# One core: skip term summed by TensorE, products read from PSUM, 7 of 32 weighings on GpSimd, direct SiLU and GELU in the end groups

## Chip, core and metric

The kernel runs on one core of a Trainium2 chip. The metric is the device time of one execution in microseconds (us), the median of repeated runs. TensorE (PE) multiplies matrices into PSUM, VectorE (DVE), ScalarE (ACT) and GpSimd (POOL) do elementwise work, SyncE (SP) issues the DMAs.

## The reference

x is 32 sequences of 128 tokens by 128 features, all float32. One layer of it:

```python
x = x + attn(rotate(x))            # rotate: pairs of rows turned by an angle per sequence
x = x + ffn(lora(x))
# attn: layernorm, then _mamba forward and on the reversed sequence, then
xc = conv4(xi) + conv_b;  u = silu(xc);  dbc = u @ x_proj.T
delta = softplus(dt @ dt_proj.T + b)           # B, C: 16 states each
h = exp(delta * A) * h + (delta * u) * B       # a scan over the tokens
y = sum_n(h * C) + u * D                       # u * D is the skip term
y = y * silu(z) @ out_proj.T
y = gelu([y_fwd, y_rev] @ reduce.T + b);  g = y @ glu.T + glu_b
attn = g[:128] * sigmoid(g[128:]) + rotate(x)
# lora: relu(x @ Wi[expert]) @ Wo[expert]
# ffn:  h = silu(x @ w1 * s1) * (x @ w2 * s2); h = gelu(h @ h1 * s); h = gelu(h @ h2 * s); h @ w3 * s
```

The inner width of the scan is 256 (two halves of 128 partitions), there are 16 states and two directions.

## The kernel before, in words

The 32 sequences are worked in nine groups: the first and the last hold two sequences (256 tokens wide), the seven between hold four (512 wide). In a group a "unit" is one state of one direction, so a group has 32 units: 16 forward (d=0), 16 reversed (d=1). A unit is a pipeline over the engines:

- GpSimd `drive`: state = du * B, L471. 128x1024 elements in a full group (two halves of 512).
- ScalarE `decays`: exp(delta * A) into one of two PSUM tiles (`bank_d`), two instructions of L614. It waits until the unit two before is done with the tile.
- VectorE `scan`: h = decay * h + state. Its result goes back into PSUM (L797) where VectorE multiplies by C next, or into SBUF (L795) where GpSimd does.
- `weigh`: times C, on VectorE from PSUM (L802) or on GpSimd (L476). The table `POOL_UNITS` names the units of a group that GpSimd weighs: 9 of 32.
- TensorE `sum_states`: eight 128x128 transposes (four in a narrow group) that add the product into `bank_y`, turned, L1076.

After 16 units a direction is finished: ScalarE copies `bank_y` to `ysum` (`copy_y`, L620), TensorE turns it back into `bank_y` (`turn_y`, L1084), VectorE adds u * D (`take_y`, two instructions, L810) into `ysum`, and then multiplies by silu(z) (`gate_y`, L819). `bank_y` is free for the other direction when `take_y` is done, and eight state buffers (`RING`) go round, so `drive` waits for the sums.

Beside the units run the "fills": matmuls of the other stages into two PSUM tiles `bank_m`, each followed by a "take" on ScalarE or VectorE that reads it. For a group: norm, uf0 uf1 ur0 ur1 (projection and convolution in one, L921), z0 z1, dbc0 dbc1, dt.., out, glu0 glu1, res, hid0-3, wo, gate0-3, up0-3, h1_0-3 (L991), h2_0-3 (L997), w3 (L1003), tok. SiLU and GELU run over whole tiles after plain takes (L570 on u, L575 on the gate, L665 on the two hidden layers), in one instruction each, to change ScalarE's table seldom: exponentials need another table than SiLU or GELU, and each change is a table load (L502).

The order of each engine's queue is fixed by tables of numbers. A time axis counts units; `FILL`, `TAKE_LAG`, `ACT_AT`, `VEC`, `GPS`, `TURN` and `LOADS` say at which unit of its group, relative to the group's first unit, each step stands. A back end of group g (FILL 37.5 to 74) runs beside the units of group g+1. Every engine walks the same axis and issues what stands there, so a shifted number moves an instruction to another place in a queue; semaphores keep the order right. SP issues the loads of B and C rows, of the weights chosen by expert (`load_selected`) and the stores in the same way.

## Time and profile before

| | us |
|---|---|
| median of 3 runs | 1112.93 (1109.14 to 1113.81) |
| the profiled execution | 1111.34 |
| its span, first to last instruction | 1109.5 |
| TensorE busy | 932.5 |
| VectorE busy | 927.7 |
| GpSimd busy | 883.1 |
| ScalarE busy | 809.0 |
| mean granted TensorE clock | 0.937 of full speed |

Busy is the time in which an instruction of the engine ran. A float32 matmul shows as two records, and so "x8" of such a line is four matmuls; a transpose is one record. Neighbouring instructions overlap by some 0.08 us, so a row's mean is that much more than what the next one waits for.

### The profile page before, as it was taken

The page shows a single profiled execution, that of the slowest core. Times are in us where ns is not written, and L with a number is a line of the kernel's source. Part 1 is how long each engine was busy: PE and PEld are TensorE (multiplying, and loading weights), DVE is VectorE, ACT ScalarE, POOL GpSimd, SP SyncE. Part 2 cuts the span into 40 slices and gives each one's busy share as a digit, 9 for nine tenths or more (in the row PEclk, how much of TensorE's full clock was granted, in tenths as well). Part 3 has the DMA queues.
Part 4 walks back from the last instruction along what each step waited for, and adds up shares of the span by engine and source line. Part 5 has one row for each costly group of instructions (what it writes and reads, how often), then busy time and mean ns, then how long its engine had stood idle before and what let it go on. Part 6 is the DMA issues. An engine that isn't in the chain of part 4 may idle for free.

```text
span 1109.5 us, 13685 instructions
## 1 busy us (share of the span) xinstructions
PE 932.5 (84%) x4240; PEld 591.1 (53%) x4240; DVE 927.7 (84%) x734; ACT 809.0 (73%) x1265; POOL 883.1 (80%) x448
## 2 busy tenths in 40 slices
PE   3498568876989989998999899998999779978876
PEld 2255345654655547545755465555655565546445
DVE  1577899999998999989998999899999999778410
ACT  3845675879688877878687968887788758676552
POOL 0675999999989898989988998899899988666200
PEclk9598679888999999999999999999999989989999
DMA  5446855465536555474536653755447453445100
GB/s 184 127 149 163 251 175 172 118 231 168 149 103 230 165 159 154 126 232 133 170 114 208 177 167 90 243 163 163 139 143 237 141 169 97 144 107 113 50 10 5
DMA packets 100840, 167.45 MB, mean 151 GB/s; under 512 B 12320, under 2 KB 36320, under 8 KB 100512
## 3 DMA queue, kind: packets, MB, share of 16 engines
q1 hardware_dynamic: 100768, 166.58, 49.5%
q8 instruction: 34, 0.56, 0.2%
...
## 4 chain that ended last, share of the span: by engine, by line
PE 36%; DVE 25%; ACT 16%; issue 16%; POOL 4%; SPq 2%; DMA 1%; DVEq 0%; ACTq 0%; POOLq 0%
DVE bank_d L797 15%; PE bank_y L1076 8%; PE bank_m L997 8%; PE bank_m L991 6%; ACT bank_d L614 5%; PE bank_m L921 4%; DVE state L795 4%; ACT L502 2%; POOL state L471 2%; PE bank_m L1003 2%; PE bank_m L933 2%; PE bank_m L939 2%; ACT hidA L665 1%; PE bank_m L953 1%; ACT hidB L665 1%
## 5 line engine op out<-in xcount | busy, mean ns | idle before, releaser
L471 POOL TENSOR_TENSOR state<-du,b_rows 128x1024 f32<-128x1024 f32 (+1 forms) x288 | 618.3, 2167 | 77.4 <-PE bank_y L1076 64.0
L797 DVE TENSOR_TENSOR_SCAN bank_d<-bank_d,state 128x1024 f32<-128x1024 f32 (+1 forms) x207 | 424.2, 2049 | 49.2 <-ACT bank_d L614 48.7
L614 ACT ACTIVATE bank_d<-delta,a_neg 128x512 f32<-128x512 f32 (+1 forms) x576 | 343.6, 633 | 82.8 <-DVE state L802 68.7
L1076 PEld LDWEIGHTS bank_y<-ident,state 128*128 128x128 f32 x2048 | 244.4, 147 | 129.6 <-issue 88.3
L1076 PE MATMUL bank_y<-ident,state 128*128 128x128 f32 x2048 | 275.1, 283 | 33.0 <-POOL state L476 16.9
L802 DVE TENSOR_TENSOR state<-bank_d,c_rows 128x1024 f32<-128x1024 f32 (+1 forms) x207 | 228.8, 1105 | 10.7 <-DMA c_rows<-bc_store 3.7
L476 POOL TENSOR_TENSOR state<-state,c_rows 128x1024 f32<-128x1024 f32 (+1 forms) x81 | 175.3, 2164 | 19.4 <-DVE state L795 18.0
L795 DVE TENSOR_TENSOR_SCAN state<-bank_d,state 128x1024 f32<-128x1024 f32 (+1 forms) x81 | 165.4, 2042 | 3.6 <-ACT bank_d L614 3.5
L997 PE MATMUL bank_m<-hidA,h_s 128*128 128x512 f32 (+1 forms) x288 | 126.1, 586 | 23.2 <-ACT hidA L665 23.2
L991 PE MATMUL bank_m<-hidB,h_s 128*128 128x512 f32 (+1 forms) x288 | 117.7, 554 | 16.2 <-DVE hidB L839 15.9
L921 PE MATMUL bank_m<-xnT,w_conv 128*128 128x508 f32 (+7 forms) x288 | 119.0, 559 | 2.0 <-ACT xnT L548 1.8
L502 ACT ACT_TABLE_LOAD x84 | 107.8, 1283 | 2.3 <-PE bank_m L953 0.8
L997 PEld LDWEIGHTS bank_m<-hidA,h_s 128*128 128x128 f32 x288 | 56.8, 207 | 72.1 <-issue 70.1
L991 PEld LDWEIGHTS bank_m<-hidB,h_s 128*128 128x128 f32 x288 | 53.2, 194 | 64.8 <-issue 40.2
L921 PEld LDWEIGHTS bank_m<-xnT,w_conv 128*128 128x128 f32 x288 | 54.5, 197 | 49.4 <-issue 43.4
L451 POOL TENSOR_TENSOR delta<-relu_dt,log_dt 128x1024 f32<-128x1024 f32 (+1 forms) x18 | 38.2, 2121 | 29.3 <-ACT log_dt L605 29.3
L659 ACT ACTIVATE hidB<-bank_m,col 128x512 f32<-128x512 f32 (+1 forms) x36 | 22.9, 635 | 43.7 <-PE bank_m L997 43.5
L953 PE MATMUL bank_m<-gy,w_glu_s 128*128 128x512 f32 (+1 forms) x36 | 23.3, 736 | 36.9 <-ACT gy L624 36.1
L939 PE MATMUL bank_m<-dbc,w_dt_s 64*128 64x512 f32 (+1 forms) x72 | 38.7, 626 | 11.6 <-ACT dbc L589 8.0
L655 ACT ACTIVATE hidA<-bank_m,col 128x512 f32<-128x512 f32 (+1 forms) x36 | 22.8, 632 | 31.6 <-PE bank_m L991 31.6
L982 PE MATMUL bank_m<-glu_a,w_s 128*128 128x512 f32 (+1 forms) x72 | 36.3, 621 | 9.1 <-ACT glu_a L649 8.2
L558 ACT ACTIVATE u_r<-bank_m,col 128x512 f32<-128x512 f32 (+1 forms) x18 | 11.5, 639 | 41.0 <-PE bank_m L921 41.0
(112 smaller groups left out, 989.9 us busy)
## 6 DMA issues: line engine op xcount, KB each, us to landing
b_rows<-bc_store SPq DMA_DIRECT2D x224, 256.0 KB, 4.7
c_rows<-bc_store SPq DMA_DIRECT2D x224, 256.0 KB, 4.7
...
```

What stands on the lines that cost most here:

```text
L471: nc.gpsimd.tensor_tensor(split(unit_state(u)), du[:, d, :, :width(g)], per_half(b_rows, u), ALU.mult).then_inc(S.bx_ready, 1)
L476: nc.gpsimd.tensor_tensor(split(unit_state(u)), split(unit_state(u)), per_half(c_rows, u), ALU.mult).then_inc(S.weighed, 1)
L502: act.preload_act_table_set(name)
L614: ins = act.activation(split(unit_decay(u))[:, h], delta[:, d, h, :width(g)], ACT.Exp, scale=a_neg[:, h, n:n + 1])
L795: dve.tensor_tensor_scan(drive, decay, drive, 0.0, ALU.mult, ALU.add).then_inc(S.unit_done, 1)
L797: dve.tensor_tensor_scan(decay, decay, drive, 0.0, ALU.mult, ALU.add).then_inc(S.scanned, 1)
L802: dve.tensor_tensor(split(unit_state(u)), split(unit_decay(u)), per_half(c_rows, u), ALU.mult).then_inc(S.unit_done, 1)
L921: ins = pe.matmul(dst, w, src, start=(m == 0), stop=(m == TAPS - 1))
L939: return pe.matmul(bank(g, f"dt{d}{h}"), w_dt_s[:, h * P:(h + 1) * P], dbc[0:DTR, :width(g)], start=True, stop=True)
L991: ins = pe.matmul(bank(g, f"h1_{f}"), h1_s[:, q, f * P:(f + 1) * P], hidB[:, q, :width(g)], start=(q == 0), stop=(q == FC - 1))
L997: ins = pe.matmul(bank(g, f"h2_{f}"), h2_s[:, q, f * P:(f + 1) * P], hidA[:, q, :width(g)], start=(q == 0), stop=(q == FC - 1))
L1076: ins = pe.matmul(bank_y[:, h, s * P:(s + 1) * P], split(unit_state(u))[:, h, s * LEN:(s + 1) * LEN], ident[:, :], start=(n == 0 and s == ...
```

## The change

1. The skip term. `take_y` goes. `skip` is a new constant of two 128x128 matrices diag(D), made on VectorE at the start (`skip_weights`). `turn_y` first multiplies it with u into `bank_y` (one matmul per half), then adds the turned sums to it. `gate_y` reads `bank_y` from PSUM and multiplies by silu(z) at once, for d=1 with both patterns reversed; `bank_y` is free when it is done.
2. The gated linear unit: `glu0` is no longer copied by ScalarE (L631); VectorE's `add_skip` reads it from PSUM and adds its bias while it multiplies.
3. `POOL_UNITS` has 7 units in place of 9: two weighings per group go from GpSimd to VectorE.
4. In group 0 the takes of u apply SiLU themselves, and in group 8 the takes of gate, h1 and h2 apply SiLU and GELU themselves; their whole-tile instructions are gone there.
5. The selected weights are loaded one sequence at a time at four places of the axis. `tok` and `cT` share a buffer.
6. All tables of the axis have other numbers, and `slot` adds offsets of its own for group 0 (`FIRST_GROUP`) and group 8 (`LAST_GROUP`).

```diff
-POOL_UNITS = (1, 4, 8, 11, 14, 18, 22, 25, 29)
+POOL_UNITS = (3, 8, 12, 17, 21, 26, 30)
...
-TURN = (19.0, 34.0)
+TURN = (19.0, 36.0)
...
-LOADS = {"x": -37.5, "bc_store": (-8.5, 0.0), "selected": 29.5, "store": 77.0}
+LOADS = {"x": -38.5, "bc_store": (-7.5, 0.0), "selected": (24.0, 26.0, 28.0, 30.0), "store": 78.0}
...
+def slot(table, g, name, k=None):
+
+    at = table[name] if k is None else table[name][k]
+    if g == 0:
+        return at + FIRST_GROUP.get(name, 0.0)
+    return at + LAST_GROUP.get(name, 0.0) if g == NG - 1 else at
...
+        def wait_u(eng, g, d):
+            if g == 0:
+                wait_taken(eng, g, *(("uf0", "uf1"), ("ur0", "ur1"))[d])
+            else:
+                eng.wait_ge(S.u_ready, 2 * (g - 1) + d + 1)
+
+        def wait_hidden(eng, g, name):
+
+            if g == NG - 1:
+                wait_taken(eng, g, *all_of(name))
+            else:
+                eng.wait_ge({"gate": S.gate_ready, "h1_": S.h1_ready, "h2_": S.h2_ready}[name], g + 1)
...
-                return act.activation(dst if d == 0 else dst[:, ::-1], bank(g, name), ACT.Identity, bias=c("conv_b", h))
+                if g == 0:
+                    use_table(SILU)
+                return act.activation(dst if d == 0 else dst[:, ::-1], bank(g, name), ACT.Silu if g == 0 else ACT.Identity, bias=c("conv_b", h))
...
             def take_wo(g):
+
+                wait(act, S.stored, 16 * g)
                 return act.activation(cT[:, :width(g)], bank(g, "wo"), ACT.Copy)
...
-                return act.activation(hidA[:, f, :width(g)], bank(g, f"h1_{f}"), ACT.Copy, scale=c("h1_s", f))
+                if g == NG - 1:
+                    use_table(GELU)
+                return act.activation(hidA[:, f, :width(g)], bank(g, f"h1_{f}"), ACT.Gelu if g == NG - 1 else ACT.Copy, scale=c("h1_s", f))
...
+            def skip_weights():
+                dve.wait_ge(S.ident_ready, 1)
+                for h in range(HALVES):
+                    ins = dve.tensor_scalar(skip[:, h], ident[:, :], c("skip_d", h), None, ALU.mult)
+                ins.then_inc(S.skip_ready, 1)
...
-            def take_y(g, d):
+            def gate_y(g, d):
                 dve.wait_ge(S.y_turned, 2 * g + d + 1)
-                wait(dve, S.gated_ready, 2 * g + d)
-                w = width(g)
-                for h in range(HALVES):
-                    dst = ysum[:, h, :w] if d == 0 else ysum[:, h, :w][:, ::-1]
-                    ins = dve.scalar_tensor_tensor(dst, (u_f, u_r)[d][:, g % 2, h, :w], c("skip_d", h), bank_y[:, h, :w], ALU.mult, ALU.add)
-                ins.then_inc(S.y_taken, 1)
...
-                dve.tensor_tensor(gated[:, d, :, :w], ysum[:, :, :w], z[:, g % 2, :, :w], ALU.mult).then_inc(S.gated_ready, 1)
+                dst, gate_z = gated[:, d, :, :w], z[:, g % 2, :, :w]
+                if d == 1:
+                    dst, gate_z = dst[:, :, ::-1], gate_z[:, :, ::-1]
+                dve.tensor_tensor(dst, bank_y[:, :, :w], gate_z, ALU.mult).then_inc(S.gated_ready, 1)
...
-                dve.tensor_tensor(x1T[:, :w], glu_a[:, :w], glu_t[:, :w], ALU.mult).then_inc(S.x1_ready, 1)
+                dve.scalar_tensor_tensor(x1T[:, :w], bank(g, "glu0"), c("glu_b", 0), glu_t[:, :w],
+                                         ALU.add, ALU.mult).then_inc(taken_of(g, "glu0"), 1)
...
-                    wait(pe, S.y_taken, 2 * g + d)
+                    wait(pe, S.gated_ready, 2 * g + d)
...
+                wait(pe, S.skip_ready, 1)
+                w = width(g)
                 for h in range(HALVES):
+                    pe.matmul(bank_y[:, h, :w], skip[:, h], (u_f, u_r)[d][:, g % 2, h, :w], start=True, stop=False, skip_group_check=True)
                     for s in range(sequences(g)):
-                        ins = pe.transpose(bank_y[:, h, s * LEN:(s + 1) * LEN], y_rows[:, h, s * P:(s + 1) * P], ident[:, :])
+                        ins = pe.matmul(bank_y[:, h, s * LEN:(s + 1) * LEN], y_rows[:, h, s * P:(s + 1) * P], ident[:, :],
+                                        start=False, stop=True, is_transpose=True, skip_group_check=True)
```

The other take functions of the last group change as `take_h1` does. What the new numbers do to the queues is shown at three places. The first is TensorE where the units of group 4 begin and the back end of group 3 is in its second hidden layer (L991 h1, L997 h2, L1076 sums, L1084 the turning, L946 out). Before:

```order
L991 MATMUL bank_m<-hidB,h_s 128x512 x4
L1076 MATMUL bank_y<-ident,state 128x128 x24
L997 MATMUL bank_m<-hidA,h_s 128x512 x4
L1076 MATMUL bank_y<-ident,state 128x128 x8
L997 MATMUL bank_m<-hidA,h_s 128x512 x4
L933 MATMUL bank_m<-u_r,w_x_s 96x512 x2
L1076 MATMUL bank_y<-ident,state 128x128 x8
L939 MATMUL bank_m<-dbc,w_dt_s 128x512
L1076 MATMUL bank_y<-ident,state 128x128 x8
L997 MATMUL bank_m<-hidA,h_s 128x512 x4
L939 MATMUL bank_m<-dbc,w_dt_s 128x512
L1084 MATMUL bank_y<-ident,ysum 128x128 x8
```

The same place in the changed kernel (L1029 h1, L1114 sums, L1035 h2, L1123 and L1125 the new turning, L984 out):

```order
L1029 MATMUL bank_m<-hidB,h_s 128x512 x12
L1114 MATMUL bank_y<-ident,state 128x128 x32
L971 MATMUL bank_m<-u_r,w_x_s 96x512 x2
L1114 MATMUL bank_y<-ident,state 128x128 x8
L1035 MATMUL bank_m<-hidA,h_s 128x512 x4
L977 MATMUL bank_m<-dbc,w_dt_s 128x512
L1114 MATMUL bank_y<-ident,state 128x128 x16
L977 MATMUL bank_m<-dbc,w_dt_s 128x512
L1035 MATMUL bank_m<-hidA,h_s 128x512 x8
L1123 MATMUL bank_y<-u_r,skip 128x512
L1125 MATMUL bank_y<-ident,ysum 128x128 x4
L1123 MATMUL bank_y<-u_r,skip 128x512
```

Between the last h1 fill and the first h2 fill there stood 24 transposes; now 40 and the two dbc matmuls stand there. The turning has two matmuls more and comes after three h2 fills, as before.

The second is ScalarE a little later, from the last take of h2 on (L659 take of h2, L665 GELU, L537 and L541 the layernorm of the group after next, L624 `gy`, the GELU of out, L614 decays). Before:

```order
L659 ACTIVATE hidB<-bank_m,col 128x512
L614 ACTIVATE bank_d<-delta,a_neg 128x512 x2
L502 ACT_TABLE_LOAD
L665 ACTIVATE hidB<-hidB 128x2048
L537 ACTIVATE shift<-neg_mean,rstd 128x1 x4
L541 ACTIVATE scaled<-xc,shift,rstd 128x128 x4
L502 ACT_TABLE_LOAD
L614 ACTIVATE bank_d<-delta,a_neg 128x512 x4
L502 ACT_TABLE_LOAD
L624 ACTIVATE gy<-bank_m,col 128x512
L502 ACT_TABLE_LOAD
L614 ACTIVATE bank_d<-delta,a_neg 128x512 x2
```

The changed kernel (L570 and L574 layernorm, L698 take of h2, L650 decays, L704 GELU, L660 `gy`):

```order
L570 ACTIVATE shift<-neg_mean,rstd 128x1 x4
L574 ACTIVATE scaled<-xc,shift,rstd 128x128 x4
L698 ACTIVATE hidB<-bank_m,col 128x512
L650 ACTIVATE bank_d<-delta,a_neg 128x512 x4
L535 ACT_TABLE_LOAD
L704 ACTIVATE hidB<-hidB 128x2048
L660 ACTIVATE gy<-bank_m,col 128x512
L535 ACT_TABLE_LOAD
L650 ACTIVATE bank_d<-delta,a_neg 128x512 x2
```

The layernorm stands ahead of the take, and `gy` directly behind the GELU of h2, so that one pair of table loads is gone.

The third is ScalarE at the end of the program, the back end of group 8 (L655 and L659 takes of h1 and h2, L575 SiLU of the gate, L652 take of the gate). Before:

```order
L649 ACTIVATE glu_a<-bank_m 128x256
L652 ACTIVATE hidA<-bank_m,col 128x256 x4
L502 ACT_TABLE_LOAD
L575 ACTIVATE hidA<-hidA 128x4x256
L655 ACTIVATE hidA<-bank_m,col 128x256 x4
L502 ACT_TABLE_LOAD
L665 ACTIVATE hidA<-hidA 128x4x256
L659 ACTIVATE hidB<-bank_m,col 128x256 x4
L665 ACTIVATE hidB<-hidB 128x4x256
```

The changed kernel:

```order
L682 ACTIVATE cT<-bank_m 128x256
L535 ACT_TABLE_LOAD
L687 ACTIVATE hidA<-bank_m,col 128x256 x4
L535 ACT_TABLE_LOAD
L692 ACTIVATE hidA<-bank_m,col 128x256 x4
L698 ACTIVATE hidB<-bank_m,col 128x256 x4
```

Each table load stands ahead of the four takes, and three whole-tile instructions are gone.

## Rows read from the trace of the kernel before

**Rows 1.** The page: busy us of each engine, and the chain by engine.

```profile
PE 932.5 (84%) x4240; PEld 591.1 (53%) x4240; DVE 927.7 (84%) x734; ACT 809.0 (73%) x1265; POOL 883.1 (80%) x448
...
PE 36%; DVE 25%; ACT 16%; issue 16%; POOL 4%; SPq 2%; DMA 1%; DVEq 0%; ACTq 0%; POOLq 0%
```

**Rows 2.** Stretches: length, busy of PE, PEld, DVE, ACT, POOL, clock, DMA.

```profile
43.20:119.00 75.80, 62.82 (x259) 40.10 (x258) 60.99 (x73) 43.94 (x90) 54.01 (x44) 0.81 0.57 167
...
360.70:480.20 119.50, 109.16 (x500) 66.75 (x499) 112.77 (x79) 96.66 (x142) 108.96 (x50) 0.97 0.53 162
...
599.70:719.20 119.50, 109.56 (x501) 66.74 (x500) 111.19 (x80) 96.49 (x142) 109.68 (x50) 0.97 0.53 164
...
958.00:1047.10 89.10, 75.91 (x339) 45.94 (x338) 64.35 (x70) 61.78 (x108) 48.70 (x40) 0.96 0.41 98
1047.10:1109.50 62.40, 45.83 (x185) 30.90 (x184) 5.44 (x12) 23.97 (x37) 0.00 (x0) 0.97 0.02 7
```

**Rows 3.** The chain in order of time, 678 to 799: start, us, what.

```profile
714.65 5.17 PE bank_m L997 x8
...
720.70 3.44 PE bank_m L997 x8
...
740.47 1.28 ACT L502
...
744.45 1.65 ACT scaled L541 x4
...
746.11 1.28 ACT L502
...
752.07 2.05 PE bank_m L953 x2
```

**Rows 4.** Groups of instructions of the whole span by shape: busy us, mean ns.

```profile
L471 POOL TENSOR_TENSOR state<-du,b_rows 128x1024 f32<-128x1024 f32 x224 | 537.2, 2420 | 32.0 <-PE bank_y L1076 31.5
...
L802 DVE TENSOR_TENSOR state<-bank_d,c_rows 128x1024 f32<-128x1024 f32 x161 | 197.0, 1224 | 5.5
L476 POOL TENSOR_TENSOR state<-state,c_rows 128x1024 f32<-128x1024 f32 x63 | 152.1, 2414 | 8.8 <-DVE state L795 7.6 <-PE bank_y L1076 1.2
...
L819 DVE TENSOR_TENSOR gated<-ysum,z 128x1024 f32<-128x1024 f32 x14 | 24.6, 1758 | 0.0
...
L827 DVE TENSOR_TENSOR x1T<-glu_a,glu_t 128x512 f32<-128x512 f32 x7 | 11.1, 1590 | 0.0
...
L810 DVE SCALAR_TENSOR_TENSOR ysum<-u_f,col,bank_y 128x512 f32<-128x512 f32 x14 | 9.8, 738 | 1.8 <-PE bank_y L1084 1.8
```

**Rows 5.** What TensorE waited for from 599.7 to 719.2: us, times, longest.

```profile
PE bank_m L953 <- ACT gy L624: 4.3, 1, 4.3
PE bank_m L997 <- ACT hidA L665: 2.5, 1, 2.5
```

**Rows 6.** Table loads (L502) from 599.7 to 719.2: length, ACT busy, clock, DMA.

```profile
599.70:719.20 119.50, 12.83 (x10) 0.97 0.53 164
```

**Rows 7.** ACT, PE and DVE before the first scan: start, us, instruction.

```profile
28.35 1.28 ACT L502 ACT_TABLE_LOAD   x1
...
30.38 1.07 PE L933 MATMUL bank_m<-u_f,w_x_s 128*96 128x256 f32 x4 [2.46 <-issue]
...
43.21 1.22 DVE L797 TENSOR_TENSOR_SCAN bank_d<-bank_d,state 128x512 f32<-128x512 f32 x1
```

**Rows 8.** ACT and PE at the end, one by one: start, us, instruction.

```profile
1059.54 1.28 ACT L502 ACT_TABLE_LOAD   x1
...
1079.74 1.06 ACT L575 ACTIVATE hidA<-hidA 128x1024 f32<-128x1024 f32 x1
...
1093.69 1.06 ACT L665 ACTIVATE hidA<-hidA 128x1024 f32<-128x1024 f32 x1
...
1096.90 0.47 ACT L659 ACTIVATE hidB<-bank_m,col 128x256 f32<-128x256 f32 x1 [2.15 <-PE bank_m L997]
...
1083.18 8.69 PE L991 MATMUL bank_m<-hidB,h_s 128*128 128x256 f32 x32 [0.62 <-DVE hidB L839]
```

More of the change, by code:

```diff
@@ L83 @@
+LAST_GROUP = {"up0": 1.0, "uf1": -0.5, "h2_2": 4.5, "delta": -1, "ur0": -0.5, "h2_0": 8.5, "h2_1": 7.5, "h2_3": 0.5,
[3 rows of a table added]
+              "bc_store": 0.5, "softplus": 1, "inputs": 0, "x1": -0.5, "normalise": -4}
+FIRST, STEP, END = -48.0, 0.5, 96.0
 FILLS = tuple(FILL)
-BY_VECTOR = ("res", "up0", "up1", "up2", "up3", "w3")
+BY_VECTOR = ("glu0", "res", "up0", "up1", "up2", "up3", "w3")
 def fill_plan():
-    order = [(UNITS * g + FILL[name], g, FILLS.index(name), name) for g in range(NG) for name in FILLS]
+    order = [(UNITS * g + slot(FILL, g, name), g, FILLS.index(name), name) for g in range(NG) for name in FILLS]
@@ L145, in build @@
         ident = sb("ident", [P, P])
+        skip = sb("skip", [P, HALVES, P])
         a_neg = sb("a_neg", [P, HALVES, NST])
@@ L317, in load_x, with load_selected @@
                 sp.dma_start(xin[:, g % 2, :m].rearrange("p s j h -> p s (j h)"), x_p[:, n:n + m]).then_inc(x_loaded[g % 2], 16)
-            def load_selected(g):
-                first = 2 * first_pair(g)
-                chosen = [sp.value_load(expert_ids[0:1, i:i + 1], min_val=0, max_val=EXPERTS - 1)
-                          for i in range(first, first + sequences(g))]
+            def load_selected(g, s):
+                seq = 2 * first_pair(g) + s
+                chosen = sp.value_load(expert_ids[0:1, seq:seq + 1], min_val=0, max_val=EXPERTS - 1)
                 if g == 0:
@@ L407, in _ @@
                     for d in range(2):
-                        if rel == LOADS["bc_store"][d]:
+                        if rel == slot(LOADS, g, "bc_store", d):
                             store_bc(g, d)
-                    if rel == LOADS["x"] and g > 0:
+                    if rel == slot(LOADS, g, "x") and g > 0:
                         load_x(g)
-                    if rel == LOADS["store"]:
+                    if rel == slot(LOADS, g, "store"):
                         store(g)
-                    if rel == LOADS["selected"]:
-                        load_selected(g)
+                    for s in range(sequences(g)):
+                        if rel == slot(LOADS, g, "selected", s):
+                            load_selected(g, s)
                 for e in range(EXPERTS):
@@ L667, in take_tok @@
             def take_tok(g):
-                wait(act, S.stored, 16 * g)
+                wait_filled(act, g, *all_of("gate"), *all_of("up"))
                 return act.activation(tok[:, :width(g)], bank(g, "tok"), ACT.Copy)
@@ L706, in _ @@
                     for d in range(2):
-                        if rel == ACT_AT["copied"][d]:
+                        if rel == slot(ACT_AT, g, "copied", d):
                             copy_y(g, d)
-                    if rel == ACT_AT["gelu"][0]:
-                        gelu(g, 1)
-                    if rel == ACT_AT["gelu"][1]:
-                        gelu(g, 2)
+                    for layer in range(2):
+                        if g < NG - 1 and rel == slot(ACT_AT, g, "gelu", layer):
+                            gelu(g, layer + 1)
                 for g, name in takes.get(at, ()):
@@ L864, in _ @@
             conv_weights()
+            skip_weights()
             for at, groups in timeline():
```

112 lines of the change are left out of this document (54 added, 58 removed), and 16 rows, old and new, of tables (FILL, FIRST_GROUP, LAST_GROUP).

## The prediction

> **What bounds the kernel now.** I read the page first. Three engines are busy for about the same share, 80 to 84%, and the chain that ended last runs over all of them: TensorE 36%, VectorE 25%, ScalarE 16% [rows 1]. No engine alone sets the time, so I looked at stretches. Between about 120 and 958 us seven full groups pass, and each takes 119.5 us. One stretch has VectorE busy for 112.8 us and another for 111.2, yet both are 119.5 long [rows 2]: a few microseconds of VectorE work more or less did not move the period. What sets it is seen in the chain of one period [rows 3]: TensorE works through the hidden layers, waits for ScalarE's table load and GELU, works on, waits for `gy` behind three more table loads, and then hands over to VectorE's scans. So the period is a ring over three queues, and the idle time left in each is small: VectorE 119.5 - 111.2 = 8.3 us, TensorE 119.5 - 109.6 = 9.9 us, GpSimd 9.8 us [rows 2].
>
> TensorE's waits are named: 4.3 us for `gy` and 2.5 us for the GELU of h1 [rows 5]. They also cost clock. Behind the GELU wait four matmuls took 5.17 us, where four took 3.44 a little later, and behind the wait for `gy` one matmul took 2.05 us against 0.86 (3.44 / 4) [rows 3]. Both are what a granted clock at the lower level, 1.2 GHz in place of 2.4, does after an idle stretch; the mean over the period is 0.97 [rows 2]. That is 1.7 + 1.2 = 2.9 us, some 3.5 with the transposes behind the second. At full clock and without its waits TensorE would need 109.6 - 3.5 = 106.1 us per period.
>
> Outside the full groups there is a head of 43 us before the first scan [rows 7], group 0 with VectorE busy in 61 of 76 us, group 8 with 64 of 89, and a tail of 62 us in which VectorE is busy for 5 and GpSimd not at all [rows 2].
>
> **The change, part by part.** VectorE, per full group. `take_y` goes: four instructions of 0.74 [rows 4], less the overlap of 0.08 each, 2.6 us. `gate_y` reads PSUM in place of `ysum`. Its rows show a mean of 1.76 us, while the multiplication of the same size that reads `bank_d` takes 1.22 [rows 4]; I price the new one at 1.22 and gain 2 x 0.54 = 1.1. The reversed patterns I cost at nothing: `take_y` wrote one direction reversed and its two forms are equally long. The GLU product drops from a mean of 1.59 us [rows 4] to the 0.74 of a `scalar_tensor_tensor` that reads PSUM: 0.9. Two weighings come over from GpSimd, 2 x 1.15 = 2.3 after overlap. Net: -2.6 - 1.1 - 0.9 + 2.3 = -2.3 us in the mean, but only about -0.8 where gate and GLU product met no slow case. VectorE's floor is then about 110.
>
> GpSimd loses 2 x 2.41 us [rows 4] per group and goes to about 105. ScalarE loses the copy of glu0, 0.69 us, and two of its ten table loads, which took 12.83 us together [rows 6], so 2.6 us: -3.3.
>
> TensorE gains the skip matmuls: four of 128x512 per full group at 0.86, +3.4 us. Its floor goes from 106.1 to 109.5. That is real work on an engine of the ring, and nothing hides it by itself.
>
> The queues are what matters most. At the first of the places that the section on the change shows, five sums and dbc now stand between the last h1 fill and the first h2 fill: 5 x 0.87 + 1.7 = 6.1 us of work, against a take, a pair of decays, a table load and the GELU of 0.6 + 1.3 + 1.3 + 1.9 = 5.1 on ScalarE. So the 2.5 us wait and its 1.7 of slow clock are covered, by work that must be done anyway. At the second place ScalarE ran 1.3 + 1.9 + 2.4 (layernorm, 1.65 of it one row [rows 3]) + 1.3 + 2.5 + 1.3 us before `gy`; now it runs 1.3 + 1.9. TensorE has five sums (4.4) and out (3.4) between the last h2 fill and the GLU fill, ScalarE two pairs of decays, table, GELU and `gy`, 0.6 + 2.5 + 1.3 + 1.9 + 0.6 = 6.9. So of 4.3 + 1.8 us there about 5 should go. VectorE's own stall there goes too: decays were held up for 1.3 + 1.9 + 2.4 + 1.3 = 6.9 us, now for 1.3 + 1.9 + 0.6 + 1.3 = 5.1, which is less than the two units (6.9 us of VectorE work) that the two `bank_d` tiles hold.
>
> Here a page of the Trainium skill prices a term otherwise. A table load takes 1.28 us in the chain [rows 3], and the next instruction follows 0.01 us later. "ScalarE: Activation LUTs", What ACT_TABLE_LOAD costs, has 1.28 us too but adds a drain of 1.38, in all 2.66 per switch. By it the two loads dropped per period would be worth 5.3 us in place of 2.6 of ScalarE; the trace shows no such gap, so I stay with 1.28.
>
> Ring: +3.4 - 4.2 (GELU) - 5 (`gy`) - 0.8 to 2.3 (VectorE) = -6.6 to -8.1. What is late next: the floors of 109.5 (TensorE) and 110 (VectorE), and three engines so near to full cannot all run without a stall; the waits of VectorE for res (1.8) and for up (0.6) stay. Bounds for the period: -9.5 (VectorE's floor of 110) and +3.4 (no wait goes, the matmuls are added). I take 115.3, -4.2, a little under halfway from 119.5 to the floor, because it is the larger part of the waits named but keeps five of slack. Seven times: -29.4.
>
> Head: before, the first dbc matmul waited for a table load and a SiLU behind the last z take; it started at 30.4 [rows 7]. Now the z fills come first, the takes apply SiLU, and dbc can start as the last u fill ends, at about 27.9, a take ahead of the table load that began at 28.35 [rows 7]: -2.5. The first scan also stands ahead of the second group's layernorm work on VectorE (3 us, which moves into idle time), of which I count 1.2; `skip_weights` adds two small instructions in front of the first layernorm, +0.3. Sum -3.4, bounds -5.5 and +0.3. Rest of group 0: less VectorE and GpSimd work but 14.8 us idle already, 0 to -8; I take -2.
>
> Group 8: TensorE-bound in its second half. Skip matmuls of 256 columns +1.7 (four of 0.43), waits less; 0 to -6, I take -2. Moving the whole-tile GELU of h1 of group 7 behind the last decays saves the load at 1059.5 [rows 8], 1.3. Tail proper: the gate SiLU and its load stood between takes and `up`, now four takes of 0.47 [rows 8] behind one load: -2.0. h1: table load and 1.06 us of GELU [rows 8] go from the path, since the load falls under the 8.7 us of h1 matmuls [rows 8]: -2.3. h2: -1.1. Tail -6.7.
>
> Sum: -3.4 - 2 - 29.4 - 2 - 6.7 = -43.5. The profiled execution took 1111.3, and 1111.3 - 43.5 = 1067.8. It lies 1.6 below the median of the runs shown, so 1069.4; I say 1070.
>
> **Rivals.** (a) TensorE takes the place of the waits: slower. For it: its queue is in order, it is on the chain for the largest share [rows 1], and the turning of d=1 now stands two units later, at the very unit of its gate on VectorE. If the turning is late, VectorE waits at the gate with no scan to do, decays stop, and the waits come back elsewhere. Against it: TensorE ran most of a unit ahead there. It decides from the point where the skip matmuls push the turning past the scan of the unit before the gate, so that the covers above fail. Price: 7 x 3.4 + 2 x 1.7 = +27 with nothing won in the periods, less 3.4 and 6.7 at the ends: 1112.9 + 27 - 10 = 1130. (b) The ends alone: covers and added matmuls cancel, period still 119.5. For it: that the period ignored 1.6 us of VectorE work. 1112.9 - 14 = 1099, and with the ends at half 1104. (c) Full cover: the period falls to 111.5, which only VectorE sets, 7 x -8 = -56, and 1112.9 - 56 - 14 = 1043. For it: all three named waits go and GpSimd has slack. Against: no period in the trace had VectorE above 94% busy. (d) The chance that the shifts of the DMAs matter: the copy of wo now waits for the store of the group before, but that is issued four units ahead; nothing changes.
>
> **How the numbers follow.** Forecast 1070: chance 0.66, of 1055 to 1090. (a) 0.08, (b) 0.17, (c) 0.09. The range that leaves out (a) and the ends of (b) and (c) is 1050 to 1101. A change under 0.5% (5.6 us) is about what a measurement of this kernel can't tell from none. Faster by more: all but (a) and the worst of (b), 0.88. Within 0.5%: milder forms of (a) where the ends cancel a longer period, 0.04. Slower: 0.08.
>
> **What would show it.** Right: periods of about 115 us; TensorE's waits for `gy` and for the GELU of h1 below 1.5 us each and its clock at 0.98 or more; ten loads per period down to eight; `gate_y` from PSUM at 1.22 us in all its rows; first scan at about 39.5 us; from the last product of a unit to the end some 55 us in place of 62. Wrong: VectorE waiting on the turning at the gate, above all for d=1; the skip matmuls at more than 0.86 us; VectorE's idle time of 8 us unchanged and only its releaser another; or a PSUM-reading gate slower than 1.22 because TensorE writes at the same time.

## The result and the profile after

The changed kernel takes 1087.05 us (median; 1085.61 to 1087.67), the kernel before in the same rounds 1113.37; the ratio is 0.9764, with a 95% interval of 0.9731 to 0.9798. The forecast was 1070, its range 1050 to 1101. The direction was right and the time lies in the range, but only about 60% of the forecast gain came. The profiled execution has a span of 1085.4 us against 1109.5.

There is one scan per unit, 32 units to a group, so the first scan of each group cuts the span into the forecast's own terms. In the profile after, VectorE's scans of unit 0 of groups 0, 1, 5, 6 and 8, and the last product (start, us, instruction, idle before it and what ended it):

```profile
39.61 1.23 DVE L841 TENSOR_TENSOR_SCAN bank_d<-bank_d,state 128x512 f32<-128x512 f32 x1 [25.33 <-POOL state L504]
...
125.49 2.29 DVE L841 TENSOR_TENSOR_SCAN bank_d<-bank_d,state 128x1024 f32<-128x1024 f32 x1
...
590.35 2.30 DVE L841 TENSOR_TENSOR_SCAN bank_d<-bank_d,state 128x1024 f32<-128x1024 f32 x1 [1.60 <-ACT bank_d L650]
...
708.74 2.30 DVE L841 TENSOR_TENSOR_SCAN bank_d<-bank_d,state 128x1024 f32<-128x1024 f32 x1 [2.21 <-ACT bank_d L650]
...
943.11 1.23 DVE L841 TENSOR_TENSOR_SCAN bank_d<-bank_d,state 128x512 f32<-128x512 f32 x1 [1.81 <-ACT bank_d L650]
...
1020.88 0.69 DVE L846 TENSOR_TENSOR state<-bank_d,c_rows 128x512 f32<-128x512 f32 x1
```

The same scans stood at 43.21, 130.65 and 960.15 in the trace before, and its last product at 1046.41. That gives:

| stretch | before | after | gain | forecast |
|---|---|---|---|---|
| to the first scan | 43.2 | 39.6 | 3.6 | 3.4 |
| group 0 | 87.4 | 85.9 | 1.6 | 2 |
| seven full groups | 829.5 (118.5 each) | 817.6 (116.8 each) | 11.9 | 29.4 |
| group 8, to its last product | 86.3 | 77.8 | 8.5 | 2 |
| last product to the end | 63.1 | 64.5 | -1.4 | 6.7 |

The seven full groups hold 17.5 us of the miss of 19.4. The prediction's 119.5 per period needs a word. Its two windows in [rows 2] were cut to equal length, 119.5, and were no periods; from first scan to first scan the groups of the kernel before took 113.9 (the first of the seven) to 120.1, 118.5 in the mean. Three of them, groups 1, 3 and 5:

```profile
130.65:244.51 113.86, 87.91 (x429) 62.09 (x428) 109.43 (x80) 84.09 (x136) 108.48 (x49) 0.87 0.59 181
363.76:483.83 120.07, 109.73 (x502) 67.00 (x501) 113.31 (x81) 96.84 (x143) 109.54 (x49) 0.97 0.54 163
603.33:722.81 119.48, 109.54 (x502) 66.75 (x501) 111.17 (x82) 96.50 (x143) 109.68 (x49) 0.97 0.53 164
```

The group with 2.1 us more of VectorE work (third number, 113.31 against 111.17) was 0.6 us longer. So "a few microseconds of VectorE work more or less did not move the period" was not shown, and VectorE was busy for 96% of group 1, where the prediction says that no period had it above 94%. In the profile after, the next two windows are full groups, the last two group 8 and the tail (columns as in [rows 2]):

```profile
355.00:473.40 118.40, 111.22 (x510) 67.28 (x509) 110.51 (x78) 93.59 (x140) 102.58 (x48) 0.99 0.55 166
...
590.40:708.70 118.30, 111.13 (x509) 67.17 (x508) 110.42 (x77) 93.48 (x140) 102.46 (x48) 0.99 0.55 166
...
943.10:1020.90 77.80, 72.15 (x326) 44.58 (x324) 60.25 (x66) 53.89 (x100) 46.31 (x39) 0.98 0.48 107
1020.90:1085.40 64.50, 50.92 (x196) 32.73 (x196) 5.34 (x10) 21.16 (x33) 0.00 (x0) 0.97 0.02 7
```

Against [rows 2], TensorE's idle time fell from 9.9 to 7.2 us and its clock rose to 0.99. VectorE is busy for 110.4, where a floor of 110 had been forecast, and idle for 7.9, nearly as long as before (8.3). Busy time per engine (the page) and who waited for whom in the period from 590.4, against [rows 5] (us, times, longest):

```profile
PE 954.6 (88%) x4312; PEld 603.0 (56%) x4312; DVE 908.1 (84%) x718; ACT 779.5 (72%) x1235; POOL 828.9 (76%) x430
```

```profile
DVE bank_d L841 <- ACT bank_d L650: 4.7, 3, 2.1
...
PE bank_m L1035 <- ACT relu_dt L631: 2.3, 2, 1.3
PE bank_m L991 <- ACT gy L660: 2.3, 1, 2.3
```

The wait for the GELU of h1 has gone, and that for `gy` fell from 4.3 to 2.3. New is TensorE's 2.3 for the takes of dt, the step sizes, ahead of two h2 fills: nearly as much as the 2.5 that went. VectorE still waits 4.7 us for its decays, 5.0 before in the group from 603.3. The pieces came out as priced, by groups of the whole span (as [rows 4]) and by the table loads of the same period (as [rows 6]):

```profile
L504 POOL TENSOR_TENSOR state<-du,b_rows 128x1024 f32<-128x1024 f32 x224 | 523.4, 2362 | 66.0 <-PE bank_y L1114 66.0
...
L857 DVE TENSOR_TENSOR gated<-bank_y,z 128x1024 f32<-128x1024 f32 x14 | 17.1, 1220 | 10.0 <-PE bank_y L1125 10.0
```

```profile
590.40:708.70 118.30, 10.26 (x8) 0.99 0.55 166
```

The gate from PSUM takes 1.22 us in the mean (1.76 before), and eight loads take 10.26 (ten took 12.83).

### The profile page after: what moved, and what is told of

Its sections match the earlier page's. It is cut to its first block, busy times and chain, and to the rows that moved or that the text cites. A ratio compares the mean times of both kernels' runs of the same rounds, so it can differ in the third digit from the quotient of the medians.

```text
span 1085.4 us, 13767 instructions
## 1 busy us (share of the span) xinstructions
PE 954.6 (88%) x4312; PEld 603.0 (56%) x4312; DVE 908.1 (84%) x718; ACT 779.5 (72%) x1235; POOL 828.9 (76%) x430
## 4 chain that ended last, share of the span: by engine, by line
PE 47%; ACT 18%; DVE 16%; issue 14%; POOL 3%; DMA 1%; SPq 0%; DVEq 0%; POOLq 0%; ACTq 0%
DVE bank_d L841 11%; PE bank_m L1029 10%; PE bank_m L959 8%; PE bank_y L1114 8%; PE bank_m L1035 6%; ACT L535 5%; ACT bank_d L650 5%; PE bank_m L1006 2%; POOL state L504 2%; PE bank_m L1014 2%; PE bank_m L1041 2%; DVE state L846 2%; DVE state L839 1%; PE bank_m L977 1%; PE bank_m L1020 1%
## 5 line engine op out<-in xcount | busy, mean ns | idle before, releaser
L504 POOL TENSOR_TENSOR state<-du,b_rows 128x1024 f32<-128x1024 f32 (+1 forms) x288 | 603.4, 2119 | 104.3 <-PE bank_y L1114 100.3
L841 DVE TENSOR_TENSOR_SCAN bank_d<-bank_d,state 128x1024 f32<-128x1024 f32 (+1 forms) x225 | 461.2, 2050 | 66.4 <-ACT bank_d L650 41.1
L650 ACT ACTIVATE bank_d<-delta,a_neg 128x512 f32<-128x512 f32 (+1 forms) x576 | 345.0, 634 | 108.9 <-DVE state L846 95.6
L1114 PEld LDWEIGHTS bank_y<-ident,state 128*128 128x128 f32 x2048 | 240.3, 146 | 82.1 <-issue 55.9
L1114 PE MATMUL bank_y<-ident,state 128*128 128x128 f32 x2048 | 262.2, 281 | 18.7 <-POOL state L509 10.4
L846 DVE TENSOR_TENSOR state<-bank_d,c_rows 128x1024 f32<-128x1024 f32 (+1 forms) x225 | 248.7, 1105 | 7.8
L509 POOL TENSOR_TENSOR state<-state,c_rows 128x1024 f32<-128x1024 f32 (+1 forms) x63 | 134.0, 2127 | 13.6 <-DVE state L839 13.3
L1035 PE MATMUL bank_m<-hidA,h_s 128*128 128x512 f32 (+1 forms) x288 | 124.6, 583 | 16.0 <-ACT relu_dt L631 8.9
L839 DVE TENSOR_TENSOR_SCAN state<-bank_d,state 128x1024 f32<-128x1024 f32 (+1 forms) x63 | 128.7, 2042 | 4.2 <-ACT bank_d L650 4.2
L959 PE MATMUL bank_m<-xnT,w_conv 128*128 128x508 f32 (+7 forms) x288 | 118.1, 560 | 6.5 <-DVE x1T L865 4.4
L1029 PE MATMUL bank_m<-hidB,h_s 128*128 128x512 f32 (+1 forms) x288 | 117.3, 561 | 2.3 <-DVE hidB L878 2.2
L1035 PEld LDWEIGHTS bank_m<-hidA,h_s 128*128 128x128 f32 x288 | 56.3, 204 | 73.4 <-issue 55.2
L1029 PEld LDWEIGHTS bank_m<-hidB,h_s 128*128 128x128 f32 x288 | 54.4, 194 | 57.9 <-issue 53.2
L698 ACT ACTIVATE hidB<-bank_m,col 128x512 f32<-128x512 f32 (+1 forms) x36 | 22.9, 635 | 37.2 <-PE bank_m L1035 36.4
L857 DVE TENSOR_TENSOR gated<-bank_y,z 128x1024 f32<-128x1024 f32 (+1 forms) x18 | 19.8, 1102 | 27.9 <-PE bank_y L1125 27.9
L469 POOL TENSOR_TENSOR rstd<-var_eps,half_power 128x4 f32<-128x4 f32 (+1 forms) x9 | 8.5, 949 | 40.2 <-issue 20.1
L1020 PE MATMUL bank_m<-cT,w_s 128*128 128x512 f32 (+1 forms) x72 | 32.6, 575 | 5.6 <-ACT hidA L687 3.8
```

Of the source, the lines that this page charges most:

```text
L504: nc.gpsimd.tensor_tensor(split(unit_state(u)), du[:, d, :, :width(g)], per_half(b_rows, u), ALU.mult).then_inc(S.bx_ready, 1)
L509: nc.gpsimd.tensor_tensor(split(unit_state(u)), split(unit_state(u)), per_half(c_rows, u), ALU.mult).then_inc(S.weighed, 1)
L650: ins = act.activation(split(unit_decay(u))[:, h], delta[:, d, h, :width(g)], ACT.Exp, scale=a_neg[:, h, n:n + 1])
L839: dve.tensor_tensor_scan(drive, decay, drive, 0.0, ALU.mult, ALU.add).then_inc(S.unit_done, 1)
L841: dve.tensor_tensor_scan(decay, decay, drive, 0.0, ALU.mult, ALU.add).then_inc(S.scanned, 1)
L846: dve.tensor_tensor(split(unit_state(u)), split(unit_decay(u)), per_half(c_rows, u), ALU.mult).then_inc(S.unit_done, 1)
```

## The experiments

All numbers are medians; a ratio is to the kernel before, timed in the same rounds, with its 95% interval. "Period" is the distance from a group's first scan to the next one's, in groups 3 to 6.

| kernel | us | ratio | period |
|---|---|---|---|
| after | 1087.1 | 0.976 (0.973-0.980) | 117.0, 118.4 |
| e1, no skip matmuls | 1089.1 | 0.976 (0.971-0.981) | 119.5-119.8 |
| e2, skip matmuls twice | 1106.5 | 0.992 (0.989-0.995) | 120.4, 121.9 |
| e3, u x D on VectorE | 1101.7 | 0.988 (0.983-0.993) | 119.7-122.0 |
| e4, no GELU in groups 0-7 | 1063.7 | 0.954 (0.949-0.959) | 113.7-114.8 |
| e5, no skip matmuls for d=0 | 1084.6 | 0.975 (0.969-0.980) | 117.0, 118.4, once 120.1 |
| e6, new code in the old order | 1149.2 | 1.032 (1.025-1.038) | 124.3-129.0 |
| e8, GpSimd units placed | 1072.4 | 0.964 (0.958-0.970) | 116.0, once 116.4 |
| e9, last group not direct | 1092.9 | 0.983 (0.977-0.989) | as after |
| e10, eight placed | 1073.5 | 0.965 (0.960-0.970) | 116.0, once 116.4 |
| e11, nine placed | 1079.3 | 0.970 (0.966-0.974) | 116.0-116.1 |
| e12, dbc back | 1120.0 | 1.005 (1.002-1.008) | 126.0-126.3 |
| e13, takes of dt, turning | 1091.6 | 0.979 (0.975-0.982) | 117.5, 118.5 |

**TensorE's work.** e1 and e2 drop and double one line of `turn_y`, `pe.matmul(bank_y[:, h, :w], skip[:, h], ...)`. e3 drops it too and puts the two `scalar_tensor_tensor` of `take_y` back ahead of the gate. e5 has:

```
+                    if d == 1:
                         pe.matmul(bank_y[:, h, :w], skip[:, h], ...)
```

> The changed kernel without the four skip matmuls per direction pair; u x D is left out of the result. Nothing else is different. Theory T (TensorE's queue sets the period: busy 111 of 117 us, its few waits only what is left of the ring): four matmuls of 0.86 us go per full group, the mean full period falls from 116.8 to about 113.4, groups 0 and 8 give 1.7 each, and 1087 becomes about 1060. Theory V (VectorE's stalls behind decays that are held up by table loads, 2.2 + 2.1 us per period, set it): less than 1 us per period, 1080 or more.

> The changed kernel with each skip matmul issued twice (u x D is added twice, so the result has it double). Theory T: +3.4 us per full period, 1087 becomes about 1114. Theory V: the added matmuls fall into TensorE's idle 6 us, +1 us or less per period, at most 1095. Both ways the pair with the kernel without them gives the slope of the time on TensorE's work.

> The changed kernel with u x D back on VectorE (two scalar_tensor_tensor per direction into ysum right ahead of the gate, which reads ysum) and no skip matmuls; the order, the GpSimd share and the end groups stay as changed. VectorE gains about 4 x 0.74 + 1 = 4 us per period, TensorE loses 3.4. Theory T: VectorE has 7 us idle, so the period falls by 2 to 3 us, total about 1068. Theory V: VectorE's work counts, the period grows by 2 to 4, total 1101 to 1115. If both are equally tight: within 5 us of 1087.

> The changed kernel with the skip matmuls of direction d=0 alone dropped (two per group; u x D of that direction is left out of the result), those of d=1 kept. Without both pairs the time was 1089, no better than 1087, and TensorE's wait for gy had grown from 2.3 to 3.7-4.1 us with 3.7 us of slow clock behind it, after which VectorE waited 3.4 us at the GLU product in place of 0.9. Theory C (the d=1 matmuls stand right ahead of that wait and fill it; taking them away only lengthens it and drops the clock): the wait for gy stays at 2.2-2.4, the periods stay at 116 to 118, total 1075 to 1087. Rival: removed work is given back wherever it stood (the ring has its length from ScalarE), periods 119.5 again and 1089.

Theory T falls with e1: 3.4 us of matmuls less per period, and the traced period grew by 1.9 in groups 3 to 6, while the total, as a ratio, is that of the kernel after. TensorE comes to the product of `gy` earlier and finds it no earlier there. In e1's trace (start, us, instruction, idle before) the wait is 4.06 us, and what follows runs at the lower clock, 1.2 GHz:

```profile
626.70 2.05 PE L991 MATMUL bank_m<-gy,w_glu_s 128*128 128x512 f32 x2 [4.06 <-ACT gy L660]
628.54 1.06 PE L943 MATMUL bank_m<-ident,scaled 128*128 128x128 f32 x4
629.39 3.55 PE L1114 MATMUL bank_y<-ident,state 128*128 128x128 f32 x16
```

```profile
646.25 0.75 DVE L865 SCALAR_TENSOR_TENSOR x1T<-bank_m,col,glu_t 128x512 f32<-128x512 f32 x1 [3.42 <-PE bank_m L991]
```

The row behind these three starts at 632.78, 6.1 us after the first. In the profile after, where the wait is 2.34 and the first row reads 1.10, the same stretch takes 3.1 us (622.00 to 625.13). So 3.0 us are lost to the clock (the 3.7 in the expectation of e5 counts the overlap of the rows as loss), and VectorE then waits 3.42 us at the GLU product in place of 0.86. e5 bears out the place: with the d=0 matmuls gone and those of d=1 kept, which stand ahead of `gy`, the wait for `gy` is 2.2 to 2.3 and three of its four periods are those of after; 1.7 us of work less bought nothing that the timing can tell. So in this ring the skip matmuls cost nothing that the timing can tell; the ratios of e1, e5 and after lie in one another's intervals, and only the traced periods (119.6 in the mean without the d=1 matmuls, 118.1 with them) speak for keeping those of d=1.

Twice as many do cost: e2 lies 19.4 us above, between V's 1095 and T's 1114. In groups 3 to 6 the period grows by 3.4, all that was added, and by 2.4 in the mean of the seven groups. The turnings come late: VectorE waits 1.9 and 2.5 us at the two gates. So neither theory holds by itself: there the first 3.4 us were free and the next were paid in full.

e3 lands at the low end of theory V: VectorE is busy for 3.6 us more per period (114.1) and the total grows by 14.6, where T had forecast a gain. But e3 also lacks the skip matmuls. Against e1, where TensorE has the same work, it is 12.5 us, half of 7 x 3.6.

**VectorE's stalls.** e4 replaces `ACT.Gelu` by `ACT.Identity` and drops `use_table(GELU)` in groups 0 to 7. e8, e10 and e11 change one line:

```
-POOL_UNITS = (3, 8, 12, 17, 21, 26, 30)
+POOL_UNITS = (2, 5, 10, 14, 18, 23, 27)            # e8
+POOL_UNITS = (2, 5, 10, 13, 17, 20, 24, 27)        # e10
+POOL_UNITS = (2, 5, 10, 13, 16, 19, 22, 25, 28)    # e11
```

> The changed kernel with Identity in place of GELU in groups 0 to 7 (gy, h1, h2), so that two excursions to the GELU table, four of eight table loads per period, go from ScalarE; GELU is left out of the result there. Instruction counts and sizes stay. Theory V: VectorE's two stalls of 2.2 and 2.1 us per period go, 7 x 4.3 = 30, about 1057. Theory T: only TensorE's wait for gy (2.2) and some slow clock behind it go, 1 to 2 us per period, 1073 to 1080.

> The changed kernel with the seven GpSimd units of a group at 2, 5, 10, 14, 18, 23, 27 in place of 3, 8, 12, 17, 21, 26, 30; nothing else. Theory V2: VectorE waits 2.1 us at unit 9 and 1.6 at unit 0 for decays held up by an excursion to the GELU table, and the unit that it has in hand meanwhile is one of GpSimd's (8 and 30), 1.15 us shorter than its own. With longer units there the waits are 1.0 and 0.4: 2.3 us per period, 7 x 2.3 = 16, about 1071. Rival: the total of VectorE's work is unchanged and the wait comes back elsewhere (turning, up): within 4 us of 1087.

> The changed kernel with eight GpSimd units per group, at 2, 5, 10, 13, 17, 20, 24, 27: one product more on GpSimd than the kernel that took 1072 with seven at 2, 5, 10, 14, 18, 23, 27. VectorE is busy for 110.7 of that kernel's 116.0. Theory V (VectorE's work and stalls are the period): 1.15 us less per period, about 1064. Rival (TensorE, busy for 110 to 111, is now the tighter one, and unit 20 as a GpSimd unit brings VectorE to the gate of d=0 earlier, where it waits for the turning 1.5 us already): the work goes and the wait grows by as much, 1070 to 1074.

> The changed kernel with nine GpSimd units per group as before, but placed at 2, 5, 10, 13, 16, 19, 22, 25, 28, off the units in hand at the GELU excursions. This undoes the share of 7 of 32 alone. Theory V: 2.3 us less per period than with seven, about 1056. Rival: GpSimd becomes late, since with every third unit its own it has 3 x 2.41 + 2.41 = 9.6 us to do while VectorE does 9.3, and VectorE waits at scans for it: 1072 to 1085.

e4 gains 23.4 us, nearer to V (30) than to T (7 to 14). An excursion here is a load of the GELU table, the GELU and the load back. e4 takes away VectorE's stalls and TensorE's wait for `gy` alike, so it prices the excursions and not one of the two waits. How a stall comes about is seen in the profile after, ScalarE first, then VectorE:

```profile
616.76 1.30 ACT L650 ACTIVATE bank_d<-delta,a_neg 128x512 f32<-128x512 f32 x2 [1.44 <-DVE state L846]
...
618.08 1.28 ACT L535 ACT_TABLE_LOAD   x1
...
619.37 1.91 ACT L704 ACTIVATE hidB<-hidB 128x2048 f32<-128x2048 f32 x1
...
621.87 1.28 ACT L535 ACT_TABLE_LOAD   x1
...
623.17 1.30 ACT L650 ACTIVATE bank_d<-delta,a_neg 128x512 f32<-128x512 f32 x2
```

```profile
616.64 2.29 DVE L841 TENSOR_TENSOR_SCAN bank_d<-bank_d,state 128x1024 f32<-128x1024 f32 x1
...
618.96 1.22 DVE L846 TENSOR_TENSOR state<-bank_d,c_rows 128x1024 f32<-128x1024 f32 x1
...
620.11 2.28 DVE L839 TENSOR_TENSOR_SCAN state<-bank_d,state 128x1024 f32<-128x1024 f32 x1
...
624.50 2.30 DVE L841 TENSOR_TENSOR_SCAN bank_d<-bank_d,state 128x1024 f32<-128x1024 f32 x1 [2.12 <-ACT bank_d L650]
```

The decays of unit 8 can start at 616.76 only, when unit 6 is done, and by the time they end, at 618.06, VectorE is already 1.4 us into unit 7. Unit 8 is one that GpSimd weighs (the scan at L839 has no product behind it), so it covers 2.3 us and not 3.45. The work in hand lasts until 622.4, 4.3 us; the decays of unit 9 end at 624.47, 6.4 us on, their own 1.3 counted. In e8 unit 8 is VectorE's own:

```profile
614.04 2.29 DVE L841 TENSOR_TENSOR_SCAN bank_d<-bank_d,state 128x1024 f32<-128x1024 f32 x1
616.36 1.22 DVE L846 TENSOR_TENSOR state<-bank_d,c_rows 128x1024 f32<-128x1024 f32 x1
618.43 2.30 DVE L841 TENSOR_TENSOR_SCAN bank_d<-bank_d,state 128x1024 f32<-128x1024 f32 x1 [0.84 <-ACT bank_d L650]
```

The two stalls, 2.1 and 1.6 to 2.2, became 0.8 and 0.7, and the total 1072.4, against 1071 expected. e8 beats both kernels; its interval of ratios lies wholly under that of the kernel after. Its period fell by 1.6 in groups 3 to 6 and 2.0 in the mean of the seven, not 2.3; e10 and e11 tell where it stopped. A period of e8, of e10 and of e11:

```profile
585.60:701.60 116.00, 109.87 (x509) 66.68 (x509) 110.61 (x78) 93.40 (x140) 102.60 (x47) 1.00 0.54 169
```

```profile
586.20:702.20 116.00, 110.08 (x510) 66.56 (x509) 109.31 (x76) 93.31 (x141) 104.71 (x49) 1.00 0.53 169
```

```profile
588.60:704.70 116.10, 110.18 (x509) 66.67 (x509) 108.39 (x76) 93.62 (x140) 107.14 (x50) 1.00 0.54 171
```

VectorE's work falls by 1.3 and 0.9 us (third number), the period stays at 116.0 to a tenth, and what is saved is waited away, for the most part at the gate of d=0: 1.5 us in e8, 2.7 in e10, 2.3 in e11, where the wait at unit 0 is 1.5 in place of 0.7. That is e10's rival. TensorE is busy for 110 us and idle for 5.9 to 6.1 in all three, and its clock is at the upper level. e11 lies 7 us above e8 outside these periods, in its rival's range: group 2 took 119.8 in place of 116.1 and group 7 115.6 in place of 111.8. Why is open; in groups 3 and 4 VectorE's wait at unit 0 ends with GpSimd's `drive`, as the rival has it.

**Order and code.** e6 sets the tables back to their values of before, 9 GpSimd units among them, with no end offsets; only the gate of d=0 stands at 20, where u x D used to be added, and not at 23.5. e12 undoes one move:

```
-"dbc1": -2.0, "dt10": -0.5, "dt11": 1.0,
+"dbc1": -0.5, "dt10": 0.5, "dt11": 1.5,
```

> The changed code in the order of before: the tables of the kernel before, its 9 of 32 products on GpSimd and no offsets for the end groups; the gate of d=0 moves from unit 23.5 to 20, where u x D used to be added, since the sums of d=1 now wait for it. Skip matmuls, gate and GLU from PSUM and the direct SiLU and GELU in the end groups stay. If the gain came from what is computed where: 1087 to 1095. If it came from the order (fewer table loads, gy behind one excursion, dbc between h1 and h2): the period stays near 119.5 or grows by the 3.4 us of matmuls less VectorE's 4.6, 1100 to 1115.

> The changed kernel with dbc and the step sizes of d=1 back at their old units (-0.5, 0.5, 1.5), so dbc stands behind the first h2 fill again and no longer covers the GELU of h1. Forecast's view of that cover: TensorE waits 0.7 to 2.5 us there again and loses 1.7 us of clock, 2.4 to 4.2 per period, 1104 to 1116. Rival, by theory V: TensorE's wait counts only as far as it reaches VectorE, whose stall at unit 0 comes from ScalarE's queue and stays the same: within 1 us per period, 1087 to 1094.

e6 took 1149, outside both expectations: the new code in the old order is 3.2% slower than the kernel before. In its period from 626.2 the `gy` wait is the old one, and a new one has appeared:

```profile
DVE x1T L858 <- PE bank_m L987: 6.8, 1, 6.8
...
PE bank_m L980 <- ACT gy L649: 4.3, 1, 4.3
...
PE bank_m L948 <- DVE x1T L854: 3.0, 1, 3.0
```

The GLU product now takes glu0 out of one of TensorE's two `bank_m` tiles itself, so the tile stays taken until the product, which needs the sigmoid. TensorE's convolution behind it waits 3.0 us, then runs at the lower clock (8 records in 5.36 us, against 3.56 a little later), and VectorE waits 6.8 for `res`. The new tables put glu0 at 42.5 instead of 41.5 and close to x1. That part was not run alone, so its share of the 62 us between e6 and after is not known; in the same period VectorE also waits 8.6 us for decays.

e12 took 1120, above both expectations. It costs 33 us, 8.5 per period in groups 3 to 6, the most of the single moves tried. But the wait for the GELU of h1, on which the forecast's view rested, comes back as 0.9 us only. The rows of e12:

```profile
615.33 0.67 ACT L630 ACTIVATE log_dt<-bank_m,col 128x512 f32<-128x512 f32 x1
...
616.63 10.08 PE L1035 MATMUL bank_m<-hidA,h_s 128*128 128x512 f32 x16 [4.89 <-ACT relu_dt L631]
...
629.34 1.23 DVE L857 TENSOR_TENSOR gated<-bank_y,z 128x1024 f32<-128x1024 f32 x1 [6.17 <-PE bank_y L1125]
```

The take of dt10 stands on ScalarE behind the copy of the sums and a decays pair that waits 2.35 us for VectorE. TensorE waits 4.89 for it, does two h2 fills in 10.08 us (7.03 for two in the tail of the profile after), comes late with the turning of d=1, and VectorE waits 6.17 at the gate. This is rival (a)'s path, opened by shifts of 0.5 to 1.5 units.

**The ends, and a last attempt.** e9 lets the last group take gate, h1 and h2 with Copy and applies SiLU and GELU to the whole tile. e13 is e8 with these edits (the table's name ahead of its entry):

```
-FILL       "dt11": 1.0,
+FILL       "dt11": 0.5,
+TAKE_LAG   "dt11": 0.5,
-ACT_AT     "copied": (18.5, 32.5)
+ACT_AT     "copied": (18.5, 33.0)
-LAST_GROUP "out": 0.5
+LAST_GROUP "out": -3.5
-                        if rel == TURN[d]:
+                        if rel == (34.0 if (g, d) == (NG - 1, 1) else TURN[d]):
```

> The changed kernel with SiLU of the gate and GELU of h1 and h2 in the last group applied to the whole tile again, behind the takes, as before; group 0 keeps its direct SiLU. Forecast's terms: +2.0 (gate), +2.3 (h1), +1.1 (h2), 5.4 in all, 1092.5. Rival: ScalarE has slack there and the tail is set by TensorE's queue until w3 of group 7, so only h1 and h2 count: about 1090.

> The kernel with the seven GpSimd units at 2, 5, 10, 14, 18, 23, 27 (1072), with two edits more. First: three kernels with seven, eight and nine GpSimd units placed off the excursions all have periods of 116.0 us, with VectorE busy for 110.7, 109.3 and 108.4, and in all TensorE idles 5.9. 1.3 and 1.0 of it is for the takes of dt10 and dt11, which stand on ScalarE behind the copy of the sums and behind a decays pair that waits 2.2 us for VectorE. So dt11 is filled and taken half a unit earlier, and the copy of d=1 stands behind the take of dt10. Theory T2 (from 116.0 on the ring closes over TensorE and these takes): both waits go, 1.5 to 2.3 us per period, total 1056 to 1062. Rival (VectorE's stalls behind the excursions still set it): periods within 0.5 us of 116.0, total 1069 to 1074. Second: in the last group the turning of d=1 stands two units earlier and the output product four, so the gate no longer waits behind two h2 fills of group 7. Expected: from the last product to the end 63.0 in place of 64.5 at most, since TensorE has all of group 7's h2 and w3 to do first and only its 1.5 us wait for gy goes; rival: the gate's wait of 15.8 us is on the path, and 6 us or more go.

e9 bears out the tail's terms: 5.8 us by the medians and 5.5 by the spans, against 5.4, with the last product at the same time as after.

e13 took 1091.6, and 1056 to 1062 or 1069 to 1074 had been expected. Both waits for the takes of dt went (0.24 and none), and T2 still fell. TensorE came to `gy` sooner and waited 2.78 us in place of 1.06, and the clock dropped there:

```profile
619.48 2.05 PE L991 MATMUL bank_m<-gy,w_glu_s 128*128 128x512 f32 x2 [2.78 <-ACT gy L660]
621.32 1.06 PE L943 MATMUL bank_m<-ident,scaled 128*128 128x128 f32 x4
```

It looks like e1 over again: TensorE's idle time per period was 6.1 (once 5.1) and is 5.5 to 6.1, more of it in one piece, and the period is 1.5 to 2.5 us longer than 116.0. In the tail VectorE's wait at the gate fell from 14.1 (e8) to 8.2 us and the tail grew, from 62.8 us to 66.4 behind the start of the last product: the second GELU of group 7 was late instead, and w3 waited 2.38 us and ran at the lower clock (5.37 us, 3.60 at the full level). So 5.9 us off the gate's wait shortened nothing. Group 8 itself took 3.6 us longer than in e8; that was not traced further. What closes the ring at 116.0 stays open: taking away the waits for dt only moved them to `gy`, which may point to the chain through ScalarE, but no run moved that chain by itself.

## Why the prediction was right in direction and too large

**Head, -3.4: right in the sum** (-3.6), in part by luck. First scan forecast at 39.5, measured 39.61. But dbc began at 28.86 and not 27.9, and the four records of the dt matmuls behind it took 1.10 us where they had taken 2.04, a gain of clock that nobody had counted. Group 0, -2: -1.6.

**Seven periods, -29.4: mis-sized, -11.9**, or -1.7 per period in place of -4.2. The -4.2 was a choice: the terms named gave -6.6 to -8.1, and some of it was kept back as slack. Step by step:

- TensorE +3.4: right as work, and what the next 3.4 would cost (e2); wrong as a cost here. "Nothing hides it by itself" did not hold: those of d=1 stand ahead of a wait, and without them the wait grows and the clock falls (e1).
- The h1 cover, -4.2: right that the wait and its slow clock go, but 2.3 us of waiting for the takes of dt stand in their place. The prediction had not named these takes, through which the same move decides more than the cover (e12).
- `gy`, -5: the wait fell by 2.0 and the slow clock behind it went nearly all, together some 3.5. The sum of 6.9 us on ScalarE against 7.8 on TensorE counted too little. The last h2 fill ends at 611.9, but its take starts 1.6 us later, behind the layernorm that now stands ahead of it, and the decays ahead of the table load first wait 1.44 us for VectorE (the row at 616.76 above). 1.6 + 1.4 + 6.9 = 9.9 against 7.8 is the wait of 2.3 but for 0.2.

```profile
608.26 3.60 PE L1035 MATMUL bank_m<-hidA,h_s 128*128 128x512 f32 x8
611.90 1.65 ACT L574 ACTIVATE scaled<-xc,shift,rstd 128x128 f32<-128x128 f32 x4
613.46 0.67 ACT L698 ACTIVATE hidB<-bank_m,col 128x512 f32<-128x512 f32 x1
```

- **"Less than the two units (6.9 us of VectorE work) that the two bank_d tiles hold": this step failed.** Two tiles do not hold two whole units of cover. The second one's decays end 1.4 us into the first, at both GELU excursions one of the two in hand was GpSimd's (8 and 30), 2.3 us and not 3.45, and the hold-up left out the 1.3 of the decays themselves: 4.3 of cover against 6.4, not 6.9 against 5.1. VectorE kept 4.7 us of waiting for decays, where 5.0 had stood before, and its idle time stayed at 8: a sign of being wrong that the prediction had named. e8 changes the placing alone: -14.6 us in all, 1.6 to 2.0 per period of the 2.5 that the forecast had too much. It took 1072.4, next to the 1070 forecast for the change without it.
- VectorE -0.8 to -2.3: right as work (busy 110.4, floor 110 forecast). That such work counts, against the prediction's first paragraph, e3 shows: half of it against e1. Of the table loads the eight take 10.26 / 8 = 1.28 us each, and the GELU behind the one at 618.08 starts at 619.37, 0.01 us after its end, as the load itself starts 0.02 after the row ahead of it. "ScalarE: Activation LUTs" of the Trainium skill, What ACT_TABLE_LOAD costs, adds a drain of 1.38; this trace again shows none. The share of 7 of 32 gave nothing in groups 3 to 6 once the units are placed (e11: same period with nine), but nine cost 3.7 us more in each of groups 2 and 7.

**Group 8 and tail, -8.7: together -7.1, with the parts the other way round.** The whole-tile GELU of h1 behind the last decays was worth more than its 1.3: the last scan waited 5.45 us for its decays before and 2.21 now. But TensorE still has the h2 fills of group 7 in front of it. Before, the first of the four began at 1043.07, ahead of the last product; now it begins at 1022.95, 1.4 us behind the product's end and after 2.67 us of waiting for that GELU, and runs at the lower clock. From the end of the last product to the take of w3 it is 26.6 us now and was 20.3. The direct SiLU and GELU then gave what was forecast (e9): from there to the end it is 37.2 us, against 42.1. The -6.7 forgot that the tail begins at TensorE's backlog and not at VectorE's last product. The first h2 fill of group 7, before and after:

```profile
1043.07 3.67 PE L997 MATMUL bank_m<-hidA,h_s 128*128 128x512 f32 x8 [2.78 <-ACT hidA L665]
1022.95 5.37 PE L1035 MATMUL bank_m<-hidA,h_s 128*128 128x512 f32 x8 [2.67 <-ACT hidA L704]
```

**Rivals.** (b), the period unchanged, is refuted: 116.8 in the mean against 118.5. (a) did not come, but e2 and e12 show its mechanism, the turning late at the gate, at 3.4 and 8.5 us per period in groups 3 to 6, so its 0.08 was not too much. (c) named VectorE as the last bound at 111.5; e4, without any GELU excursion in groups 0 to 7, came to 114.3 only.
